# Feed-forward layers of a one-core kernel: the second product moved two chunks behind the first, and the next group's normalisation moved forward by one chunk

## The reference

```python
def shift_token(t):
    t1, t2 = jnp.split(t, 2, axis=-1)
    t2 = jnp.pad(t2, ((0, 0), (1, 0), (0, 0)))[:, :-1]
    return jnp.concatenate([t1, t2], axis=-1)
...
x = x + o @ wo                      # end of the local attention
h = shift_token(x)
mu = h.mean(-1, keepdims=True)
var = h.var(-1, keepdims=True)
h = (h - mu) / jnp.sqrt(var + 1e-05) * lg + lb
h = h @ w1 + b1                     # 256 -> 2 * 682
a, g = jnp.split(h, 2, axis=-1)
h = a * jax.nn.gelu(g, approximate=False)
x = x + h @ w2 + b2                 # 682 -> 256
```

## Time and profile before

| | before |
|---|---|
| median of three runs | 2353.12 us |
| profiled execution, span | 2356.8 us |
| PE busy | 2160.7 us, 92% of the span |
| PEld busy | 1832.9 us, 78% |
| DVE busy | 1660.1 us, 70% |
| ACT busy | 1021.5 us, 43% |
| POOL busy | 378.4 us, 16% |
| mean granted clock of TensorE | 0.965 of full speed |
| feed-forward of layer 0 | about 1340 to 1587 us of the span |
| feed-forward of layer 1 | about 2120 us to the end |

### The profile page before, as it was taken

One profiled execution on the slowest core, in us unless ns is written; L12 is line 12 of the kernel. 1 busy time (PEld: TensorE's weight loads), 2 busy tenths in 40 slices (PEclk: granted clock), 3 DMA queues, 4 the chain that ended last, 5 costly groups with the idle time before them and its releaser, 6 DMA issues. The chain is left out here.

```text
span 2356.8 us, 42795 instructions
## 1 busy us (share of the span) xinstructions
PE 2160.7 (92%) x13920; PEld 1832.9 (78%) x13920; DVE 1660.1 (70%) x4826; ACT 1021.5 (43%) x2371; POOL 378.4 (16%) x209
## 2 busy tenths in 40 slices
PE   6799899999999599999999699987999999987998
PEld 6688788788788478888888577765888888876887
DVE  5546546546456678888888577776888888866777
ACT  3332232223232256666666333333666666652333
POOL 0000000000000022323232111112323323311111
PEclk9899999999999799999999799997999999998999
DMA  7100000000000200000000100001000000000011
GB/s 249 38 1 1 2 1 1 2 1 1 2 1 1 96 3 4 4 4 4 4 4 3 54 10 10 9 10 51 5 3 4 4 4 3 4 6 19 14 41 39
DMA packets 42344, 42.43 MB, mean 18 GB/s; under 512 B 8496, under 2 KB 36869, under 8 KB 42248
## 3 DMA queue, kind: packets, MB, share of 16 engines
q1 hardware_dynamic: 40114, 35.90, 4.7%
q10 hardware_dynamic: 2134, 5.26, 0.6%
HBM read 32.76 MB, written 8.39 MB: 17 GB/s over the span
## 5 line engine op out<-in xcount | busy, mean ns | idle before, releaser
L860 ACT ACTIVATE l_probs<-l_probs,l_negmax 128x256 f32<-128x256 f32 x512 | 253.2, 498 | 38.4 <-DVE l_negmax L937 38.4
L1077 PE MATMUL ps<-l_v,l_probsT 128*128 128x64 f32 x2048 | 252.3, 277 | 0.5 <-ACT l_probsT L866 0.5
L1077 PEld LDWEIGHTS ps<-l_v,l_probsT 128*128 128x128 f32 x2048 | 241.8, 194 | 6.5 <-ACT l_probsT L866 1.0
L825 POOL TENSOR_TENSOR l_rot<-l_t,l_t 128x1024 f32<-128x1024 f32 x64 | 152.3, 2379 | 296.7 <-DVE l_t L973 296.7
L107 PE MATMUL ps<-local_w_hi,l_xT 128*128 128x512 f32 x384 | 168.4, 438 | 24.7 <-DVE l_xT L922 24.7
L829 POOL TENSOR_TENSOR l_rot<-l_rot,l_rnorm 128x1024 f32<-128x1024 f32 x64 | 122.1, 1907 | 428.6 <-DVEq L997 428.6
L107 PE MATMUL ps<-attn_w_hi,attn_xT_hi 128*128 128x512 f32 x392 | 168.7, 430 | 12.7 <-issue 10.1
L1068 PE MATMUL ps<-ident,l_probs 128*128 128x128 f32 x1024 | 150.7, 280 | 19.4 <-ACT l_probs L860 17.1
L384 ACT ACTIVATE attn_exp<-ps 128x512 f32<-128x512 f32 x130 | 77.7, 599 | 205.6 <-PE ps L109 205.6
L1068 PEld LDWEIGHTS ps<-ident,l_probs 128*128 128x128 f32 x1024 | 113.6, 141 | 64.2 <-ACT l_probs L860 52.6
L108 PE MATMUL ps<-attn_w_lo,attn_xT_hi 128*128 128x512 f32 x392 | 158.2, 404 | 0.0
(11 more groups left out here) (199 smaller groups left out, 5658.4 us busy)
## 6 DMA issues: line engine op xcount, KB each, us to landing
tok_x<-x SPq DMA_DIRECT2D x16, 512.0 KB, 4.5
m_shifted<-shifted SPq DMA_DIRECT2D x18, 256.0 KB, 2.8
shifted<-x SPq DMA_DIRECT2D x64, 64.0 KB, 1.5
out<-x SPq DMA_DIRECT2D x8, 512.0 KB, 3.8
ffn_w_raw<-ffn_w SPq DMA_DIRECT2D x6, 640.0 KB
local_w_raw<-ffn_wqkv SPq DMA_DIRECT2D x4, 768.0 KB, 5.2
h<-txt SPq DMA_DIRECT2D x4, 512.0 KB, 4.8
attn_w_raw<-attn_Wq ACTq DMA_DIRECT2D x1, 1024.0 KB, 7.5
```

Source lines behind the costliest of these rows:

```text
L825: nc.gpsimd.tensor_tensor(rot[:], t1[:], t2[:], ALU.add).then_inc(s.summed.sem, 1)
L860: last = nc.scalar.activation(v, v, ACT.Exp, bias=nb[:, h:h + 1], scale=8.0, accum_out=rsum[:, h:h + 1])
L1077: last = nc.tensor.matmul(ps[:, 7, h * DH:(h + 1) * DH], pt[:, pair % 2, (2 * e + w) * P:(2 * e + w + 1) * P], vv[:, w, h * DH:(h + 1) * D ...
```

## The change

PE issues `down` two chunks behind `up` instead of one: in a group it is up(0), down(4) of the group before, up(1), down(5) of the group before, up(2), down(0), and so on. The transposes of the next group stand behind chunk 3, not chunk 4.

On DVE everything about the next group moves forward by one chunk: variance behind chunk 0 (was 1), deviation behind 1 (was 2), normalise behind 2 (was 3), scaled in chunk 3 (was 4), normed_lo ahead of chunk 4 (was 5). `stats` of the group after the next moves to the end of the group. The residual of the group before moves from chunk 0 to chunk 1. ACT's `normed_hi` moves from chunk 4 to chunk 3. POOL's code is the same.

Since `stats` now runs one group ahead, SP fetches one more piece of `shifted` at the end, and DVE computes one more set of statistics; neither is used.

```diff
+            sp.wait_ge(*s.normed.room(NG + 1, 2))
+            sp.dma_start(sh[:, 1], A.scratch[0:GT, :].rearrange("(j p) c -> p j c", p=P)).then_inc(s.sh_in[1].sem, 16)
...
-                sp.wait_ge(*s.sh_in[r].after(16 * (NG // 2 + 1 - r)))
+                sp.wait_ge(*s.sh_in[r].after(16 * (NG // 2 + 1)))
...
-                    if c == 4:
+                    if c == 3:
                         normed_hi(1 - r, g + 1)
...
-                    if c == 5:
+                    if c == 4:
                         normed_lo(1 - r, g + 1)
                     between = None
-                    if c == 0 and tail:
+                    if c == 1 and tail:
                         between = lambda: residual(g - 1)
-                    if c == 4:
+                    if c == 3:
                         between = lambda: scaled(g + 1)
                     hidden(c, C * g + c, between)
                     if c == 0:
-                        stats(g + 1, 1 - r)
+                        norm.variance(nc, chain)
                     if c == 1:
-                        norm.variance(nc, chain)
+                        norm.deviation(nc, chain)
                     if c == 2:
-                        norm.deviation(nc, chain)
-                    if c == 3:
                         normalise(g + 1, 1 - r)
+                    if c == C - 1:
+                        stats(g + 2, r)
...
+            stats(1, 1)
...
-                    if c:
-                        if c == 1 and tail:
+                    if c >= 2:
+                        if c == 2 and tail:
                             pe.wait_ge(*s.y_done.after(G * g))
-                        down(c - 1, C * g + c - 1)
+                        down(c - 2, C * g + c - 2)
                     elif tail:
-                        down(C - 1, C * g - 1)
-                    if c == 4:
+                        down(C - 2 + c, C * g - 2 + c)
+                    if c == 3:
                         transposes(g + 1)
...
+            down(C - 2, C * NG - 2)
             down(C - 1, C * NG - 1)
```

## The result

The changed kernel takes 2394.72 us (median of four runs, 2392.34 to 2398.22). The kernel before, run beside it, takes 2356.76 us (2353.01 to 2361.01). The ratio is 1.0167, with a 95% interval of 1.0146 to 1.0189: slower. The forecast was 2392 us; by the medians of kernels run side by side the change costs 38.0 us, where the forecast's sum was 39.3. The profiled execution has a span of 2396.4 us against 2356.8.

What follows compares the result with a forecast made beforehand. PE, the fullest engine, was taken to bound the kernel, with waits for u_lo in the feed-forward blocks. The terms 19.1 + 0 + 24 - 1 - 2.8 = +39.3 us on the median of 2353.1 gave 2392 us, range 2363 to 2406.

Steps and rivals of the forecast that it cites:

- Where PE waits before, and what could be won: Feed-forward blocks: PE waits for u_lo; the change can win at most 1.45 us a group in layer 1, 3.5 in layer 0.
- The waits for `u_lo` go: Both layers: u_lo has one more up and down, 4.22 us, before it is wanted, so its waits go.
- Layer 1: POOL holds the deviation, PE waits 4.2 us before the transposes: groups 29.4 us against 26.67, +19.1 us over 7 groups.
- Layer 0: POOL holds normalise, PE waits 3.4 us before the transposes: groups 28.7 us against 28.69, 0 over 8 groups.
- The clock: Half clock on PE behind each of 15 waits of 3.4 to 4.2 us costs 1.6 us: +24 us.
- Small terms: Layer 1's first group loses its short waits, -1 us; the wait at each block's end is covered, -2.8 us; others 0.
- A: Rival on PE's clock: half clock comes for few of these waits, +15, 2368 us; chance 0.25.
- B: Rival, both layers: POOL does not hold the small instructions long, every PE wait goes, -42, 2311 us; chance 0.07.
- C: Rival: normalise is not held in layer 0, -28 there; layer 1 as forecast; -2 in all, 2351 us; chance 0.08.
- D: Rival: only one POOL instruction holds the deviation in layer 1, wait 1.8 us, +16 in all, 2369 us; chance 0.08.
- E: Rival: more half clock than one stretch behind each wait, twice the stretch in layer 1, +11, 2403 us; chance 0.04.

Runs made afterwards that it cites:

- e1: The changed kernel with POOL's work of each group waiting for u_lo of chunk 4 (layer 1) or chunk 3 (layer 0): 2318.03 us, ratio 0.9841.
- e5: The changed kernel with PE running matmuls nobody reads while it waits before the transposes, 16 in layer 1, 10 in layer 0: 2375.91 us, ratio 1.0073.
- e6: The changed kernel without POOL's second instruction of each group in layer 1, which adds the layers' input to m_xb: 2366.42 us, ratio 1.0042.
- e3: The changed kernel with down one chunk behind up as before, so only the normalisation is a chunk earlier: 2387.96 us, ratio 1.0138.

## Why the prediction was right, point by point

- **Where PE waits before, and what could be won.** A group without waits was put at 25.2 us. e1 runs at 25.20.
- **The waits for `u_lo` go.** They did, in every steady group.
- **Layer 1.** Transposes were put 12.6 us behind down(5), a wait of 4.2 us, a group of 29.4 us without the clock. Measured: 4.0 to 4.3 us, and 29.61 us with the clock kept full (e5). The held instructions are the first and the third of the deviation, as worked out, with 2.40 and 2.34 us.
- **Layer 0.** A wait of 3.4 us was forecast; it is 3.0. Groups without half clock take 1491.36 - 1462.99 = 28.37 us instead of 28.7. The held instructions are two of normalise, as forecast, but the two long rows add 1.44 + 2.45 - 2 x 0.34 = 3.2 us, not the 3.5 that I took.
- **The clock.** This term was mis-sized in both directions. I took 1.6 us behind each of 15 waits, 24 us. In layer 1 each of the seven waits of 4 us had half clock, and it cost 1.8 us each. In layer 0 the waits of 3.0 us had it at some and not at others: the group behind the wait at 1433.08 takes 29.91 us, the one behind 1462.99 takes 28.37, so a stretch costs 1.5 us, and the mean over six groups is 0.8 instead of 1.6. Layer 0 came out at +5.1 us where the terms of the prediction made 11, layer 1 at +32.3 where they made 28. Over the six steady groups of layer 0 the clock costs 6 x (1.6 - 0.8) = 4.8 us less than forecast, and the shorter wait 6 x (28.7 - 28.37) = 2.0 us less. Over six groups of layer 1 the clock is 1.3 us above the forecast (6 x 0.22) and the rest of the group another 1.3 us (6 x (29.61 - 29.4)). The errors of the two layers, -6.3 and +4.4 us, and the 2.2 us that lie elsewhere nearly cancel: that the total met the forecast of 39 us so closely is in part luck.
- **Small terms.** The first group of layer 1 did not lose its waits: 1.64 us stand before its transposes (2160.60). This is part of the 4 us that layer 1 is above the forecast. In layer 0 the first group waits 4.40 us, longer than the steady ones (1374.17). The prediction had missed that in a first group there is no down of a group before, so PE reaches the transposes two downs earlier. In e1, with POOL out of the way, 1.36 us (layer 0) and 1.62 us (layer 1) of these two waits are left. The wait of 1.56 us at a block's end is gone in both layers, as forecast.
- **The rivals.** A (no price for the clock) falls by e5: about 19 us. B (the promise holds) falls with the profile after, and e1 shows what it would take. C falls: normalise is held, 1.44 and 2.45 us. D falls: two POOL instructions hold two of DVE; e6 shows what one alone does, 2366 us where D was put at 2369. E (a second stretch at half clock behind each wait of layer 1) is so at two of the seven waits, which have 6.8 us at half clock; the mean cost of 1.8 us a wait is far from the 3.2 that E takes. The rule of the Trainium skill cited there (page "SBUF — State Buffer", section "Who interferes with whom") agrees with the trace: the `tensor_scalar` form of normalise is held, 1.44 and 2.45 us against 0.34.

What was argued and not tried: that the hold is a lock on a port. The runs show who stands still, under whom, and for how long; they would look the same for another resource that both engines need for a whole instruction.

## What to carry to other kernels

When a step is moved on an engine that shares a resource with another, list what will stand beside the other engine's long instructions, not only how late the step itself may be: here 5.3 us of POOL's work, which had lain beside statistics and held one `u_lo` for 1.4 us (2.10 instead of 0.68), came to lie beside ten small instructions, and held two of them for 2.2 us each, 4.4 in all. Giving POOL a later start, one wait, turned the same reordering from 1.7% slower into 1.6% faster. And one long wait of PE costs more than its length: price the matmuls behind it at half clock (here 1.8 us behind a wait of 4.0 to 4.3).

## What the runs showed of the hardware that was not expected

- PE does the same work faster if it is given useless work to do while it waits: 16 and 10 extra matmuls a group made the kernel 18.8 us shorter (e5).
- PE waits of 1.6 to 2.2 us in layer 1 of e6 brought no half clock in any steady group; waits of 3.0 us in layer 0 brought it in some groups, in turns; waits of 4.0 to 4.3 us brought it every time. In layer 0 of the kernel before the waits of 1.8 to 1.9 us were followed by one all the same in three of eight groups; one is in the earlier trace rows.
- In all seven steady groups of layer 1 of the changed kernel a held instruction of the deviation (four columns) ends 0.02 to 0.03 us behind POOL's, and exactly one more slips between two POOL instructions that stand 0.16 us apart. A held normalise instruction (128 columns) ends 0.08 us behind POOL's, a held `u_lo` (512 columns) 0.54 us behind, at 2226.52 against 2225.98.
- How many tiles an instruction reads does not decide alone: of two four-column instructions under the same POOL instruction in e3, `TENSOR_REDUCE` (L141) passes in 0.17 us and `TENSOR_SCALAR` (L142) is held for 2.20, though each reads one tile.
